# Row-moving indirect DMAs of a routed FFN: each waits for the last but one

## The reference

```python
x = x + 0.5 * ffn(layernorm(x), router_w, rms_w, w1, w2, rms_w_s, w1_s, w2_s)
x = x + attention(layernorm(x), w_qkv, w_proj)      # 16 heads of 8, causal, ALiBi
x = x + 0.5 * ffn(layernorm(x), router_w, rms_w, w1, w2, rms_w_s, w1_s, w2_s)

def ffn(x):                      # 4096 tokens of 128
    gates = softmax(x @ router_w)                    # 14 routed experts
    top_v, top_i = top_k(gates, 2)                   # each token: its best 2, weights normalised
    routed = sum of top_v * expert(top_i)(x)
    return routed + shared_expert_0(x) + shared_expert_1(x)

def expert(x):
    h = x * rsqrt(mean(x * x) + eps) * rw            # rw: one row for each expert
    return silu(h @ W1) @ W2                         # 128 -> 256 -> 128
```

## Time and profile before

| | |
|---|---|
| median of 3 runs | 1360.35 us (1357.62 to 1366.43) |
| the profiled execution's own time | 1365.05 us |
| its span, first to last instruction | 1363.2 us |
| mean granted TensorE clock | 0.847 of full speed |
| PE busy | 994.5 us, 73% of the span |
| DVE busy | 771.5 us, 57% |
| ACT busy | 500.5 us, 37% |
| POOL busy | 365.6 us, 27% |
| scatters, L641 | 128 DMAs |
| gathers, L653 | 128 DMAs |

### The profile page before, as it was taken

One profiled execution on the slowest core, in us unless ns is written; L12 is line 12 of the kernel. 1 busy time (PEld: TensorE's weight loads), 2 busy tenths in 40 slices (PEclk: granted clock), 3 DMA queues, 4 the chain that ended last, 5 costly groups with the idle time before them and its releaser, 6 DMA issues.

```text
span 1363.2 us, 22089 instructions
## 1 busy us (share of the span) xinstructions
PE 994.5 (73%) x6993; PEld 602.4 (44%) x6993; DVE 771.5 (57%) x1851; ACT 500.5 (37%) x825; POOL 365.6 (27%) x423
## 2 busy tenths in 40 slices
PE   4725393578178899999999999989896344936844
PEld 3514393576033334443444444434344134925733
DVE  6525262374067777868787768878634242614604
ACT  1101161343001555645565455655551012513401
POOL 5744406202700021001300040001125453071070
PEclk9767596699666999989999999999996575966977
DMA  9211142222600113220313023300000112422321
GB/s 324 85 43 39 60 133 79 75 85 73 156 2 2 40 37 77 46 50 3 99 37 72 3 63 73 72 3 3 3 1 31 39 41 69 126 78 78 115 53 38
DMA packets 84263, 85.39 MB, mean 63 GB/s; under 512 B 11732, under 2 KB 73444, under 8 KB 81700
## 3 DMA queue, kind: packets, MB, share of 16 engines
q1 hardware_dynamic: 50950, 55.28, 15.4%
q0 software_dynamic: 8192, 16.79, 4.3%
q10 hardware_dynamic: 25024, 12.06, 3.0%
HBM read 52.48 MB, written 37.45 MB: 66 GB/s over the span
## 4 chain that ended last, share of the span: by engine, by line
PE 42%; issue 24%; DVE 11%; another core or an unknown queue 10%; POOL 5%; DVEq 3%; ACT 2%; POOLq 1%; DMA 1%; ACTq 0%; SPq 0%
PE banks L1563 8%; PE banks L1533 8%; PE banks L1546 6%; PE banks L1472 4%; PE banks L1459 3%; DVE nmax L1176 3%; POOL region_a L653 2%; POOL region_c L653 2%; PE banks L1398 2%; PE banks L1382 2%; DVE work L1063 2%; PE banks L1536 2%; PE banks L1549 1%; ACT work L863 1%
## 5 line engine op out<-in xcount | busy, mean ns | idle before, releaser
L863 ACT ACTIVATE work<-banks 128x1024 f32<-128x1024 f32 (+3 forms) x384 | 297.5, 812 | 267.6 <-PE banks L1549 199.4
L1176 DVE TENSOR_REDUCE nmax<-banks 128x1 f32<-128x512 f32 (+3 forms) x432 | 275.5, 668 | 59.9 <-PE banks L1533 33.2
L1063 DVE SCALAR_TENSOR_TENSOR work<-work,banks 128x512 f32<-128x512 f32 x156 | 106.9, 686 | 290.5 <-issue 146.2
L1533 PE MATMUL banks<-ks,qs 75*128 75x512 bf16 (+3 forms) x576 | 188.5, 356 | 29.6 <-DVE nmax L1176 17.0
L1472 PE MATMUL banks<-region_c,work 128*128 128x128 f32 x736 | 109.4, 296 | 100.2 <-DVE work L1063 78.3
L1398 PE MATMUL banks<-w,work 128*128 128x128 f32 x512 | 80.1, 311 | 132.6 <-DVE xs L1071 74.2
L1563 PE MATMUL banks<-work,vaug 128*9 128x512 f32 (+3 forms) x1536 | 165.1, 503 | 0.0
L1546 PE MATMUL banks<-qs,ks 78*128 78x512 bf16 (+3 forms) x576 | 157.4, 335 | 2.9 <-ACT work L863 2.9
L1398 PEld LDWEIGHTS banks<-w,work 128*128 128x128 f32 x512 | 75.7, 221 | 172.7 <-DVE xs L1071 84.1
L641 POOL DMA_INDIRECT sorted_x<-region_b,pos x128 | 124.0, 969 | 103.0 <-DVEq L1043 65.2
L1472 PEld LDWEIGHTS banks<-region_c,work 128*128 128x128 f32 x736 | 98.7, 208 | 106.0 <-DVE work L1063 68.4
(11 more groups left out here) (160 smaller groups left out, 1236.3 us busy)
## 6 DMA issues: line engine op xcount, KB each, us to landing
xld<-sorted_x SPq DMA_DIRECT2D x92, 128.0 KB
sorted_y<-ysb ACTq DMA_DIRECT2D x92, 128.0 KB
qs<-q_scr SPq DMA_DIRECT2D x36, 192.0 KB
ks<-k_scr SPq DMA_DIRECT2D x36, 192.0 KB
q_scr<-qp SPq DMA_DIRECT2D x20, 256.0 KB
k_scr<-kp SPq DMA_DIRECT2D x12, 256.0 KB
region_c<-q_scr SPq DMA_DIRECT2D x12, 192.0 KB
region_c<-k_scr SPq DMA_DIRECT2D x12, 192.0 KB
```

The costliest lines, as they stand in the source:

```text
L863: nc.scalar.activation(pT[s % 2][pair][:, :, 0:w], ps_s[pair][:, :, 0:w], ACT.Exp).then_inc(s_e, 1)
L1063: nc.vector.scalar_tensor_tensor(uu[slot], th[slot], 1.0, ps_h[slot], ALU.add, ALU.mult).then_inc(o.u, 1)
L1176: nc.vector.tensor_reduce(dst, ps_1[n % 2][:, 0:len(pieces) * w].rearrange("p (h j) -> p h j", j=w), axis=AXX, op=ALU.max, negate=True).th ...
L1533: last = mm(dst, qs[g][0:PASS1_ROWS, h, it * P:(it + 1) * P], ks[g][0:PASS1_ROWS, h, j0:j0 + w], start=True, stop=not diagonal)
```

## The change

Two semaphores, `s_moved[0]` and `s_moved[1]`, serve all 256 indirect DMAs of the program in turn: DMA number n adds to `s_moved[n % 2]`. Ahead of DMA n, POOL waits until that semaphore stands at `16 * (n // 2)`, that is, until DMA n - 2 has landed. The numbers run through the program in POOL's order (`SCATTERS` and `GATHERS` give the place of each burst). SP and DVE wait for the counts that their rows correspond to, on both semaphores. No instruction changes its place or its engine, and nothing is computed differently. The core of the diff:

```diff
+MOVES = TOP_K * GT
+MOVE_SEMS = 2
+SCATTERS, GATHERS = (0, 1, 4, 5), (2, 3, 6, 7)
...
+        s_moved = [sem(f"rows_moved{i}") for i in range(MOVE_SEMS)]
+
+        def moved(first, count):
+
+            return [(s_moved[i], 16 * (sum(n % MOVE_SEMS == i for n in range(first + count))))
+                    for i in range(MOVE_SEMS) if any(n % MOVE_SEMS == i for n in range(first, first + count))]
...
                 for r in range(GROUPS):
-                    sp.wait_ge(o.sc[r], 16 * TOP_K * GT)
+                    for s, count in moved(MOVES * SCATTERS[GROUPS * f + r], MOVES):
+                        sp.wait_ge(s, count)
...
                     for k in range(TOP_K):
+                        n = MOVES * SCATTERS[GROUPS * f + r] + TOP_K * t + k
+                        if n >= MOVE_SEMS:
+                            pool.wait_ge(s_moved[n % MOVE_SEMS], 16 * (n // MOVE_SEMS))
                         nc.gpsimd.indirect_dma_start(
                             out=sorted_x[r], out_offset=bass.IndirectOffsetOnAxis(ap=pos[r][:, k, t:t + 1], axis=0),
-                            in_=xh_tile(r * GT + t), in_offset=None).then_inc(o.sc[r], 16)
+                            in_=xh_tile(r * GT + t), in_offset=None).then_inc(s_moved[n % MOVE_SEMS], 16)
...
                     for k in range(TOP_K):
+                        n = MOVES * GATHERS[GROUPS * f + r] + TOP_K * t + k
+                        pool.wait_ge(s_moved[n % MOVE_SEMS], 16 * (n // MOVE_SEMS))
                         nc.gpsimd.indirect_dma_start(
...
-                            ).then_inc(o.got[r][t // BLOCK], 16)
+                            ).then_inc(s_moved[n % MOVE_SEMS], 16)
...
-                dve.wait_ge(ffn[f].got[r][j], 16 * TOP_K * BLOCK)
+                for s, count in moved(MOVES * GATHERS[GROUPS * f + r] + TOP_K * BLOCK * j, TOP_K * BLOCK):
+                    dve.wait_ge(s, count)
                 dve.drain()
```

More of the change, by code:

```diff
@@ L375, in build @@
             o.pos = sem(f"f{f}_rows_known")
-            o.sc = [sem(f"f{f}_scattered{i}") for i in range(GROUPS)]
             o.xl = [sem(f"f{f}_rows_in{i}") for i in range(2)]
@@ L382, in build @@
             o.ys = [sem(f"f{f}_rows_out{i}") for i in range(2)]
-            o.got = [[sem(f"f{f}_gathered{i}_{j}") for j in range(BLOCKS)] for i in range(GROUPS)]
             o.add = sem(f"f{f}_block_added")
             ffn.append(o)
+        s_moved = [sem(f"rows_moved{i}") for i in range(MOVE_SEMS)]
+        def moved(first, count):
+            return [(s_moved[i], 16 * (sum(n % MOVE_SEMS == i for n in range(first + count))))
+                    for i in range(MOVE_SEMS) if any(n % MOVE_SEMS == i for n in range(first, first + count))]
         s_mv = sem("a_stats")
```

## The result

The changed kernel took a median of **1265.33 us** (1261.21 to 1266.45, 4 runs), the kernel before, beside it, 1360.32 (1357.62 to 1366.43, 4 runs): a ratio of **0.9291, 95% interval 0.9257 to 0.9325**. I had forecast 1385, in a range of 1290 to 1405.

What follows compares the result with a forecast made beforehand. Indirect DMA bursts, with PE, DVE and ACT frozen beside them, were taken to delay the whole kernel. Waits of 2 (scatters) + 12 (gathers) + 10 (fourth burst) = +24 us gave 1385 us, range 1290 to 1405.

Steps and rivals of the forecast that it cites:

- the freeze: PE, DVE and ACT nearly without work during bursts of indirect DMAs while POOL issues; cause not named by any row.
- the rival: The freeze loosens, chance 0.30; the quoted words are the prediction's argument against it.
- the 159.5 us: Ten stretches of indirect DMA bursts with PE, DVE and ACT nearly idle; given as the most that unfreezing gives back.
- Scatter wait, +2: Wait ahead of 128 scatters: spacing goes from 1.265 to 1.28 us, costing 2 us, bounds 0 and 13.
- Gather wait, +12 for three bursts: Wait ahead of gathers in three bursts of 32: spacing becomes 1.38 us, costing 12 us, bounds 5 and 19.
- Fourth burst, +10: Gather burst beside SP's transfers: five DMAs under way become two, costing 10 us, bounds 4 and 19.
- my upper case: Fourth burst: one DMA takes 6 us whatever stands beside it, starts 3 us apart, costing 19 us.
- Waits on SP and DVE, 0: SP and DVE wait for two counts instead of one, reached with the same burst as before: no cost.
- The freeze loosens: Rival, chance 0.30: pace of issue decides, and gaps in it let the other engines through; middle 1290 us.
- The wait never binds: Rival, chance 0.23: POOL's usual 0.3 us covers it; scatters 0, gathers 5, fourth burst 4 or less; 1360 to 1370 us.

Runs made afterwards that it cites:

- e8: The changed kernel with one semaphore, so each indirect DMA waits for the last: 1435.17 us (one run), ratio 1.28, where the kernel before does not freeze.
- e2: The kernel before with the wait for the last but one ahead of scatters only: 1116.99 us, ratio 0.9984, where the kernel before does not freeze.
- e9: The kernel before with the wait for the last but one ahead of the fourth burst's gathers only: 1115.74 us, ratio 0.9982, in the free condition.
- e6: The kernel before, unchanged, run again for its trace where it does not freeze: 1124.96 us in its one profiled run, 1117.88 median of 13 runs.
- e1: The kernel before with the wait for the last but one ahead of gathers only: 1154.28 us, ratio 1.0325, where the kernel before does not freeze.
- e4: The changed kernel with a one-column power on POOL ahead of each scatter: 1200.66 us, ratio 1.0752 to the kernel before, in the free condition.
- e11: The kernel before with a one-column power on POOL ahead of every second gather, no wait: 1144.41 us against 1119.16, ratio 1.0196, free condition.
- e10: The changed kernel with three semaphores in turn, at most three DMAs under way: 1126.56 us, ratio 1.0078 to the kernel before, free condition.
- e7: The changed kernel with four semaphores in turn, at most four DMAs under way: 1118.06 us, ratio 0.9989 to the kernel before, free condition.

## Why the prediction was wrong, step by step

**The sign: the freeze.** The step that failed is, in the words of the rival, "in seven bursts of eight the cap of two is kept already", from which I concluded that a limit of two could not loosen a freeze that it does not change. Counted by packets it holds in the third burst (after 8 us 5 have moved of 7 issued, after 20 us 15 of 16). But the wait is for the landing, not for the last packet, and my own price for a gather, 2.9 us until the next may start against two spacings of 2.5, says that today a third one starts before the first is seen to have landed. So the limit did change the gather bursts, by my own sum, and they are the ones that are free after it. The forecast also treated the engines as a fixed backdrop: I priced the waits with idle engines beside them, and asked only at 0.30 whether the engines would work. They did, in four bursts, and that gave back 94.7 us net of the waits' own cost. The remaining frozen stretches of scatters are why it is not more: there the wait binds 25 times and the bursts grow by 1.0 to 1.7 us only. And the 159.5 us that I gave as the most there is to gain are ten stretches only; the free condition shows 240.

**Scatter wait, +2.** Frozen condition: bursts 1.0 to 1.7 us longer each, some 5 us in all against 2 in my sum, and inside my bounds of 0 to 13. The price of 2.56 us from start to start was right within 0.06 (2.50 in e8). Free condition: 95 waits and 17 us of longer bursts, no cost (e2).

**Gather wait, +12 for three bursts.** Mis-sized by a factor of two or more: the three grew by 31.5 us in the frozen condition (51.8, 50.0 and 46.6 us, where they were 39.0, 39.1 and 38.8) and by 26 in the free one. I took the landing time, 2.6 us, from the last DMA of frozen bursts, when nothing else was moving. The time from issue to landing of the kernel before in the free condition, gather bursts 3, 4 and 8 (smallest, median, greatest):

```profile
DMA to landing us min/median/max: 2.7/3.3/3.7
...
DMA to landing us min/median/max: 2.5/7.0/9.6
...
DMA to landing us min/median/max: 2.4/2.5/3.5
```

Beside the pairs' transfers it is 3.3 us, and two under way in 3.3 + 0.3 is a spacing of 1.8; measured was 51.5 / 31 = 1.66 in the third burst of the change, 1.49 in the eighth, against my 1.38. In the frozen condition what came to run beside the third burst took the DMA share from 0.25 to 0.47, so a price read beside standing engines was too low there. For the eighth burst it isn't the landing that I had wrong (2.5 us), and what makes the spacing 1.49 there is open.

**Fourth burst, +10.** Its length grew by 23 us, above my upper case of 19; its cost on the kernel, where it could be measured by itself, is nothing (e9, free condition). I had written that nothing covers it. That was read off the frozen trace, where PE was busy 8.8 of 42 us beside it. Where PE works, the attention's first part covers it. What I called attention's small pieces beside it are loads of 192 KB and stores of 256 KB (18 and 3 in this burst of e6).

**Waits on SP and DVE, 0.** Not measured by itself. The 6 us by which the change and e1 cost more than their bursts grow may lie here or elsewhere.

**Sum.** In the free condition, +24 forecast and +32 (26 to 39) measured. That this is near is luck: it is another condition than the one forecast, and the terms are wrong in both directions, 26 to 32 + 0 + 0 where I had 12 + 10 + 2. (1360.35 + 24 is 1384, not 1385.) In the frozen condition the waits' cost is more than paid by what the freed engines do.

**The rivals.** The freeze loosens came true, with 1290 as its middle and 1265 measured. Its mechanism, gaps in the issue that let other engines through, is **not shown**. Three things stand: (1) in the frozen condition, exactly the bursts where the wait binds often are free, which can be cause or effect; (2) in the free condition the same DMAs at the same pace, with as many under way and no limit, freeze nothing (the fourth burst); (3) so what is needed besides a burst is something that differs between the conditions and that no row names. Whether the limit frees the engines, or the longer spacing, or whether another burst would do, was to be told by e1 to e4 and e11, and none of them met the frozen condition. It stays open. The wait never binds was wrong for gathers (76 of 128) and, for scatters, right about the cost though not about the binding (25 and 98 of 128).

## What to carry to other kernels

When a trace shows engines standing still beside one engine's work, ask of every price read there whether it would hold if they moved: a landing time or a cover taken from a frozen stretch is not the one that comes after. A limit on what is under way has a dose: in the free condition one cost 28%, two 2.9%, three 0.8%, four nothing, so where a limit is wanted, the loosest that does its work is the one to take. Whether three or four would loosen the freeze is not shown. And before a stall that nothing in the program explains is traded for a wait, look at the same kernel at another time or on another chip: this change is worth 7% in one condition and costs 3% in the other.

## What the runs showed of the hardware

- The same kernel took 1360 us in one condition and 1118 in another. PE is busy 8.8 us of the fourth burst in one and 35.0 in the other, with 32 DMAs issued in 39.0 us in both. In the frozen one a limit of two under way brought 1265 us, in the free one it cost 32 us.
- An indirect DMA of 64 KB from SBUF to DRAM takes 2.2 us from issue to landing (median in e8); one from DRAM to SBUF 2.5 us in the eighth burst of e6, 3.3 beside the pairs' loads and stores of 128 KB, 7.0 beside SP's transfers of 192 and 256 KB (up to 9.6).
- With one under way, 2.50 us from start to start when writing DRAM, 2.8 when writing SBUF (e8). POOL itself is good for one in 1.25 us, so at least two must be under way to keep it busy; with traffic beside them three still cost 0.8% and four nothing (e10, e7).
